# Values' projections in halves and an earlier divide at the start, half output tiles at the end, eight buffers of x

## The reference

```
Q = x @ w_q.T;  K = ctx @ w_k.T;  V = ctx @ w_v.T          (split in 16 heads of 32)
attn = softmax(Q K^T / sqrt(32))                            (64 keys for each row)
out = (attn V) @ w_o.T + b_o + x
y = (out - mean) * rsqrt(var + 1e-5) * ln_gamma + ln_beta
```

## Time and profile before

| | us |
|---|---|
| three runs: lowest, median, highest | 577.16, 578.68, 580.47 |
| the profiled execution | 577.46 |
| its span, first to last instruction | 575.7 |
| PE busy in it | 539.5 (94%) |
| DVE busy | 462.1 (80%) |
| POOL busy | 428.6 (74%) |
| ACT busy | 394.6 (69%) |

### The profile page before, as it was taken

The page is one execution under the profiler, slowest core; times in us unless marked ns, Lnnn a source line. Parts: engine busy times, 40 slices in busy tenths (PEclk is TensorE's granted clock), DMA queues, the critical chain, the costliest instruction groups (busy, mean ns, idle before and its releaser), DMA issues.

```text
span 575.7 us, 12718 instructions
## 1 busy us (share of the span) xinstructions
PE 539.5 (94%) x4522; PEld 379.5 (66%) x4522; DVE 462.1 (80%) x870; ACT 394.6 (69%) x735; POOL 428.6 (74%) x397
## 2 busy tenths in 40 slices
PE   8899879999999999999999999999999999998771
PEld 7566457676777676677677776767776776775450
DVE  7767549888889888889888889888888888888534
ACT  7537647777777777777777777777777777666522
POOL 0804466888888888888888898878888888666575
PEclk9999899999999999999999999999999999999876
DMA  9335314343344433443244433343344322222212
GB/s 323 117 89 146 99 28 135 97 130 96 117 127 121 128 97 94 127 123 119 74 124 126 117 118 117 97 130 98 123 125 126 101 72 77 82 83 64 71 64 91
DMA packets 74111, 63.23 MB, mean 110 GB/s; under 512 B 46528, under 2 KB 46528, under 8 KB 74048
## 3 DMA queue, kind: packets, MB, share of 16 engines
q1 hardware_dynamic: 74048, 62.42, 36.3%
HBM read 39.58 MB, written 16.78 MB: 98 GB/s over the span
## 4 chain that ended last, share of the span: by engine, by line
PE 81%; DVE 5%; DMA 4%; POOL 3%; issue 2%; SPq 2%; ACT 2%; POOLq 0%; ACTq 0%; DVEq 0%
PE ps_o L403 27%; PE ps_q L397 26%; PE ps_c L362 10%; PE ps_s L335 7%; DMA max_rows<-max_turned 3%; PE ps_q L275 3%; PE ps_s L345 3%; PE ps_o L275 2%; SPq L209 2%; PE ps_s L275 2%; POOL y L847 1%; POOL y L845 1%; DMA x_raw<-in_x 1%; PE ps_c L282 1%; DVE q_lo L636 1%
## 5 line engine op out<-in xcount | busy, mean ns | idle before, releaser
L397 PE MATMUL ps_q<-x_hi,wq_lo 64*128 64x512 f32 x448 | 187.0, 417 | 0.0
L403 PE MATMUL ps_o<-wo_hi,c_lo 64*128 64x512 f32 x448 | 185.9, 415 | 0.0
L397 PE MATMUL ps_q<-x_hi,wq_hi 64*128 64x512 f32 x448 | 175.9, 393 | 0.0
L397 PE MATMUL ps_q<-x_lo,wq_hi 64*128 64x512 f32 x448 | 175.4, 391 | 0.0
L403 PE MATMUL ps_o<-wo_hi,c_hi 64*128 64x512 f32 x448 | 175.0, 391 | 0.0
L403 PE MATMUL ps_o<-wo_lo,c_hi 64*128 64x512 f32 x448 | 173.2, 387 | 0.0
L397 PEld LDWEIGHTS ps_q<-x_hi,wq_lo 64*128 64x128 f32 x448 | 82.5, 184 | 66.8 <-DVE z L720 46.1
L845 POOL TENSOR_TENSOR y<-y,gamma_row 128x512 f32<-128x512 f32 x62 | 79.9, 1289 | 62.2 <-ACT y L540 62.2
L817 POOL TENSOR_TENSOR x_lo<-xT_raw,x_hi 128x512 fp32r<-128x512 f32 x60 | 77.5, 1291 | 35.3 <-ACT x_hi L475 28.4
L823 POOL TENSOR_TENSOR c_lo<-c_raw,c_hi 128x512 fp32r<-128x512 f32 x64 | 82.6, 1291 | 19.4 <-ACT c_hi L475 19.4
L397 PEld LDWEIGHTS ps_q<-x_hi,wq_hi 64*128 64x128 f32 x448 | 82.6, 184 | 9.3
(11 more groups left out here) (97 smaller groups left out, 1101.9 us busy)
## 6 DMA issues: line engine op xcount, KB each, us to landing
xT_raw<-in_xT SPq DMA_DIRECT2D x64, 256.0 KB, 3.3
x_raw<-in_x SPq DMA_DIRECT2D x64, 256.0 KB, 2.9
out<-y SPq DMA_DIRECT2D x64, 256.0 KB, 2.3
max_rows<-max_turned SPq DMA_DIRECT2D x256, 16.0 KB
ctx_raw<-in_ctxT SPq DMA_DIRECT2D x4, 256.0 KB, 4.0
wk_raw<-in_wkT SPq DMA_DIRECT2D x4, 256.0 KB, 4.2
wq_raw<-in_wqT SPq DMA_DIRECT2D x4, 256.0 KB, 5.2
wv_raw<-in_wvT SPq DMA_DIRECT2D x4, 256.0 KB, 6.6
```

The lines of the kernel that those rows point to most:

```text
L397: return nc.tensor.matmul(ps_q[:, 0, :], w[l][half, k, dims], x_[r][half, qc % 2, k, :], start=(half is lower and k == 0 and step == 0), s ...
L403: return nc.tensor.matmul(ps_o[:, 0, :], cx[l][half, k, tile], wo[r][half, k, :], start=(half is upper and k == 0 and step == 0), stop=(ha ...
```

## The change

At the start, `project_values` is called in halves of k: the first half of the first one before the first scores, and then one half in each of slots 0 to 6, ahead of `subtract_max` and not behind it. `divide` moves ahead of `queries_to_lo` on DVE. `max_rows` gets two buffers, and with them two semaphores. `x_raw` and the small tiles of the norm get eight buffers; x is loaded earlier (slots 2 to 5, and `load_x(t)` in the loop in place of `load_x(t - 4)`), and no load of x is left in the tail. In the tail the output tiles go in halves around `score`, `subtract_max` and `combine_values`; tiles 62 and 63 go to banks of ps_s; DVE finishes tiles 57, 58, 62 and 63 in place of 62 and 63.

```diff
-    BY_DVE = 2
+    BY_VECTOR = (57, 58, 62, 63)
...
-        max_rows = sb("max_rows", [P, CHUNK], fp32r)
+        max_rows = sb("max_rows", [P, 2, CHUNK], fp32r)
-        x_raw = sb("x_raw", [P, 4, DM], fp32)
+        x_raw = sb("x_raw", [P, 8, DM], fp32)
...
         def out_bank(i):
+            if i >= TILES - 2:
+                return ps_s[:, i % 2, :]
...
             def load_x(i):
-                wait(sp, z_done, i - 3)
+                wait(sp, z_done, i - 7)
             def fill_max_rows(n):
-                wait(sp, shifted_done, n)
+                wait(sp, shifted_done, n - 1)
...
-                if t in (2, 3):
+                if 2 <= t <= 5:
                     load_x(2 * t - 4)
                     load_x(2 * t - 3)
...
-            for t in range(OUT_LAG + 1, SLOTS + 1):
-                load_x(t - 4)
+            for t in range(OUT_LAG + 1, SLOTS):
+                load_x(t)
...
-            for i in range(SLOTS - OUT_LAG - 1, TILES):
-                if i + 5 < TILES:
-                    load_x(i + 5)
+            fill_max_rows(SLOTS - 1)
+            for i in (55, 57, 56, 58, 59, 60, 62, 61, 63):
                 store(i)
```

PE, the start:

```diff
             project_queries(0)
+            project_values(0, first_half)
             for t in range(OUT_LAG):
                 score(t)
                 project_queries(t + 1)
+                if t == 0:
+                    project_values(0, second_half)
+                else:
+                    project_values((t + 1) // 2, first_half if t % 2 else second_half)
                 if 1 <= t < OUT_LAG - 1:
                     subtract_max(t - 1)
-                if 1 <= t <= KT:
-                    project_values(t - 1)
                 if t >= 2:
                     combine_values(t - 2)
```

PE, the tail (the new list):

```diff
+            subtract_max(61); project_output(56, first_half); score(63)
+            project_output(56, second_half); project_output(57, range(KT)); combine_values(61)
+            project_output(58, first_half); subtract_max(62); project_output(58, second_half)
+            combine_values(62); project_output(59, first_half); subtract_max(63)
+            project_output(59, second_half); combine_values(63)
+            project_output(60, range(KT - 1)); project_output(61, range(KT - 1))
+            project_output(62, first_half); project_output(60, (KT - 1,))
+            project_output(61, (KT - 1,)); project_output(62, second_half); project_output(63, range(KT))
```

ACT, the start and the tail (the new list):

```diff
-                if 1 <= t <= KT:
-                    even_values(t - 1)
+                if t % 2 == 0:
+                    even_values(t // 2)
...
+            normalise(54); exponentiate(61); log_sums(60); invert_sums(60); negate_max(62)
+            invert_deviation(55); normalise(55); context_to_hi(60); log_sums(61); negate_max(63)
+            invert_sums(61); exponentiate(62); context_to_hi(61); log_sums(62); invert_sums(62)
+            exponentiate(63); invert_deviation(56); context_to_hi(62); normalise(56)
+            log_sums(63); invert_sums(63); invert_deviation(57); context_to_hi(63)
+            invert_deviation(58); invert_deviation(59); normalise(59); invert_deviation(60)
+            normalise(60); invert_deviation(61); normalise(61); invert_deviation(62); invert_deviation(63)
```

DVE, the start and the tail (the new list):

```diff
                 fold_halves(t)
+                if t >= 3:
+                    divide(t - 3)
                 queries_to_lo(t + 1)
                 turn_max(t)
-                if t >= 3:
-                    divide(t - 3)
-                if 1 <= t <= KT:
-                    odd_values(t - 1)
+                if t % 2 == 0:
+                    odd_values(t // 2)
...
+            statistics(55); turn_scores(62); half_maxima(62); fold_halves(62); turn_scores(63)
+            turn_max(62); divide(60); half_maxima(63); fold_halves(63); add_residual(56)
+            turn_max(63); divide(61); add_residual(57); statistics(56); add_residual(58)
+            statistics(57); divide(62); statistics(58); add_residual(59); finish(57); divide(63)
+            statistics(59); finish(58); add_residual(60); statistics(60); add_residual(61)
+            statistics(61); add_residual(62); statistics(62); finish(62)
+            add_residual(63); statistics(63); finish(63)
```

POOL, the start, the loop and the tail (the new list):

```diff
-                if t >= 5:
-                    add_bias(t - 5)
                 if t >= 3:
                     context_to_lo(t - 3)
+                if t >= 4:
+                    add_bias(2 * t - 8)
+                    add_bias(2 * t - 7)
...
-                add_bias(i + 3)
+                add_bias(t - 1)
...
+            scale(54); add_bias(62); add_bias(63); shift_mean(55); scale(55)
+            context_to_lo(60); context_to_lo(61); shift_mean(56); context_to_lo(62); scale(56)
+            context_to_lo(63)
             for i in (59, 60, 61):
                 shift_mean(i)
                 scale(i)
```

More of the change, by code:

```diff
@@ L118, in cross_attention_kernel @@
         xT_loaded = [sem(f"xT_loaded{k}") for k in range(KT)]
-        x_loaded = [sem(f"x_loaded{s}") for s in range(4)]
+        x_loaded = [sem(f"x_loaded{s}") for s in range(8)]
         x_biased = sem("x_biased")
@@ L307, in project_queries, with project_values @@
                 mm.then_inc(q_product, 1)
-            def project_values(b2):
-                wait(pe, even_values_done, 2 * b2)
-                wait(pe, odd_values_done, 2 * b2)
+            def project_values(b2, ks):
+                if ks[0] == 0:
+                    wait(pe, even_values_done, 2 * b2)
+                    wait(pe, odd_values_done, 2 * b2)
                 keys = slice(b2 * P, (b2 + 1) * P)
-                for k in range(KT):
+                for k in ks:
                     if b2 == 0:
@@ L341, in subtract_max @@
                     pe.wait_ge(select_filled, 16 * 8)
-                pe.wait_ge(max_rows_filled, 64 * (n + 1))
+                pe.wait_ge(max_rows_filled[n % 2], 64 * (n // 2 + 1))
                 for pair in range(2):
                     rows = slice(64 * pair, 64 * (pair + 1))
-                    mm = nc.tensor.matmul(ps_s[:, 2 * (n % 2) + pair, :], select[rows, :], max_rows[rows, :],
+                    mm = nc.tensor.matmul(ps_s[:, 2 * (n % 2) + pair, :], select[rows, :], max_rows[rows, n % 2, :],
                                           start=False, stop=True, skip_group_check=True)
@@ L536, in normalise @@
             def normalise(i):
[L537 to L538 removed]
+                s, c = i % 4, i % 8
+                act.wait_ge(shift_done, by_scalar(i) + 1)
                 wait(act, y_stored[s], 16 * (i // 4))
[L540 to L541 removed]
+                nc.scalar.activation(y[:, s, :], z[:, s, :], ACT.Identity, bias=shift[:, c:c + 1],
+                                     scale=rstd[:, c:c + 1]).then_inc(normed_done, 1)
             def exponentiate(n):
@@ L782, in _ @@
             statistics(57)
-            divide(SLOTS - 2)
+            divide(62)
             statistics(58)
             add_residual(59)
+            finish(57)
+            divide(63)
             statistics(59)
-            divide(SLOTS - 1)
-            for i in (60, 61):
-                add_residual(i)
-                statistics(i)
-            for i in (62, 63):
-                add_residual(i)
-                statistics(i)
-                finish(i)
+            finish(58)
+            add_residual(60)
+            statistics(60)
+            add_residual(61)
+            statistics(61)
+            add_residual(62)
+            statistics(62)
+            finish(62)
+            add_residual(63)
+            statistics(63)
+            finish(63)
         @block.gpsimd
```

214 lines of the change are left out of this document (108 added, 106 removed).

## The result

The kernel after the change takes 559.94 us (median of four runs, 559.06 to 560.87), against 577.92 for the kernel before, run beside it (median of four; the 578.68 above is that of the first three of them). The ratio is 0.9682, with a 95% interval of 0.9646 to 0.9718: about 18 us, or 3.2%, faster. The profiled execution took 559.06, its span 557.3, against 557.7 forecast for the span.

The account below looks back on a forecast made before the run. PE bounds the loop, which keeps its 440.5 us; only 33 us of idle in start and tail can be won. Start 7.1 and tail 10.9 gained: 578.68 - 18.0 = 560.7 us, range 555.5 to 566.5.

Parts of the forecast that it names:

- Rival 4: Loop: POOL's list waits for x in every slot, lengthening the period; at 0.4 us per slot 583 us; chance 0.03.
- the collision: Start: max_rows fills queue behind w_o transfers on two DMA engines, losing 3.8 of the 10.9 us gained.
- fill 3: Start: max_rows fill of slot 3 lands at about 55.3, needed at 52.8, so PE waits 2.5 us.
- fill 4: Start: max_rows fill of slot 4 lands at about 63.2, needed at 62.3, so a wait of 0.9 us.
- Rival 1: Start: no collision, fills and w_o land in time; first interleaved tile at 68.7, kernel 556.9 us; chance 0.18.
- the loop at 64.9 + 7.6: End of the start: slot 6 starts at 64.9 and the loop 7.6 later, at 72.5.
- rival 3: Start: PE at 1.2 GHz and ACT held by w_o; gains only 4, first tile at 75, 563.8 us; chance 0.13.
- the pace of 6.9: Start: from slot 2 on, a slot takes 8.28 - 1.4 = 6.9 us with values in halves.
- c_raw waits: Start: PE's waits of 2.81 and 3.25 us, from `divide` standing behind `queries_to_lo`; none over 0.3 afterwards.
- c_lo(63): Tail: done at 547.7 against 553.2 before, 5.5 us won; 27.6 after the last loop matmul.
- 12, if finish(57) does not hold divide(63) (1.5 less): Tail's upper end: gain of 12 us, if DVE's divide(63) need not wait 1.5 for finish(57) ahead of it.
- Rival 2: Tail: the new order waits for itself, two waits grow by 2.5 each; tail gains 6, 565.6 us; chance 0.20.

Follow-up runs that it names:

- the start alone: Kernel before with only the start's new order on PE, ACT and DVE, one max_rows buffer, four x buffers, old tail: 571.56 us, ratio 0.9877.
- `divide` late: Changed kernel with `divide` behind `turn_max` again in the start, values still in halves: 563.47 us, ratio 0.9744.
- values late: Changed kernel with the values' projections whole and behind `subtract_max` again, `divide` still early: 559.67 us, ratio 0.9674.
- one max_rows: Changed kernel with all fills into one max_rows buffer, the fill's wait shifted accordingly: 559.45 us, ratio 0.9688.
- the last run above: Changed kernel with w_o in transfers of 32 rows, rstd(62) ahead of normalise(61), tile 63's residual and statistics ahead of finish(62): 554.85 us, ratio 0.9606.
- the tail alone: Changed kernel with the start's order of before (values whole behind `subtract_max`, `divide` late): 567.27 us, ratio 0.9809.

## Why the prediction was right, and where its sizes were off

The total came out closer than its parts: the start gained 6.0 where 7.1 was forecast, the tail 12.1 where 10.9 was, and that the two misses nearly cancel is luck.

**The loop** kept its time: 440.23 against 440.46. Rival 4 is out.

**The start: the mechanism was right, and shown.** The slots ran at 6.98 until the fill of slot 3 was late, behind w_o. Giving w_o transfers of 32 rows removed both waits and gave 4.1 us from the first scores to the first tile, against the 3.8 that the prediction took off for the collision. The rule cited from the Trainium skill ("DMA: Bandwidth & Descriptors", the section on why a DMA increments its semaphore by 16) fits: 32 can be divided by 16, and the same bytes no longer held up what was behind them (3.1 to landing in place of 8.1 for x). Rival 1, no collision, gave 68.7 for the first tile; it became true at 69.11 only when the form of w_o was changed.

**The start's sizes.** The wait for fill 3 was 1.90 and not 2.5, for fill 4 it was 1.44 and not 0.9: their sum is 3.3 against 3.4. The rest of the 1.1 by which the start fell short (6.04 against 7.1) lies at its two ends: this execution's first queries ended 0.33 later (19.98, not 19.65), and from slot 6 to the first tile it took 8.3 where 7.6 was forecast, with 1.57 of waiting for the odd values' copy. The term that was mis-sized is "the loop at 64.9 + 7.6". Most of its 0.7 is w_o once more, by way of ACT, which waited for the last quarter of it ahead of `queries_to_hi`:

```profile
70.08 0.63 ACT L495 ACTIVATE wo_hi<-wo_raw 128x512 fp32r<-128x512 f32 x1 [1.95 <-DMA wo_raw<-in_woT]
```

DVE's low part of the queries, and all behind it in that slot, waited for that; with w_o in 32 rows the same stretch took 7.7. The forecast had put this hold of ACT at nothing and left it to rival 3.

**Rival 3** (more lost) came true in its mechanisms in some executions, and in none at its price. ACT's hold was there, as just said. Other kernels with this start's order had 2.68, 2.10 and 2.48 for the same fill. Behind the 2.68 and the 2.48 the granted clock fell (means of 0.84 and 0.72 from 55 to 60), behind the 2.10 and the 1.90 it did not. From the first scores the first tile took 52.3 and 52.0 with the fall, 51.6 and 52.1 without, so that it cost 0.7 at most, and the first tile was in none of them at the 75 of rival 3. With the fall the wait for the next fill was gone, without it it was 1.23 and 1.44: the later fill had its wait in the time that PE lost.

**Which part of the start pays** is the step that failed in its attribution. The prediction gave the pace of 6.9 to the halves and named `divide` as the cure of the c_raw waits beside them. The runs show that `divide`'s place alone gives the same first tile (73.52), and that the halves without it lose 2.7 of the gain from the first scores (3.5 by the medians). Beside the early `divide` the halves pay only once w_o is out of the way. The sum had both halves of the edit in it and needed no split between them, and so the total came out right.

**The tail** gained 12.1 where 10.9 was taken and 11.1 worked out. `finish(57)` does hold divide(63), in its place as said; its second step took 0.75, not the 1.44 taken from the earlier trace rows, since it began just ahead of POOL's step of `scale(56)`, and POOL's was the longer one for it (1.81). PE did not fall to the lower clock in this tail; in four executions of other kernels with the same PE list it did, and where nothing else differed their tails were 1.2 longer. That it stayed up here was luck. c_lo(63) was 1.3 earlier than forecast. The step "12, if finish(57) does not hold divide(63) (1.5 less)" was wrong in what it promised: with the hold taken away, in the one order that was tried, the tail was 0.8 longer. The rounds of 3.9 and 4.1 and rstd(62) behind `normalise(61)` ended last, as said; but of the 2.67 that DVE waits there only 1.1 can be had by the earlier rstd, because DVE's steps then take 1.5 longer beside POOL's. Rival 2 is out: no two waits grew.

Of the tail's 12.1, the x buffers with their earlier loads give 4.7 and the remaining 7.4 belong to the new lists with DVE's two more tiles. These were not run apart, so how the 7.4 is split between the half tiles on PE, the fill ahead of the stores and tiles 57 and 58 on DVE stays open.

## What to carry to other kernels

Look at the first dimension of every transfer: here one of 2 in place of 32 made what was issued behind it pay, and it began to cost when a faster schedule took the slack. When two edits of an order come together, price each without the other: here one moved line gave all, and the larger edit beside it paid nothing until a third thing was mended. In a tail, an earlier result on one engine is worth what the other engines' lists leave of it: look at all of them, and at which steps lengthen each other, before pricing a wait at its length. And compare stretches of single executions only where the clock and the waits ahead of them are alike.

## What the runs showed of the hardware

**DVE and POOL lengthen each other's steps.** `SCALAR_TENSOR_TENSOR` of 128x512 fp32 on DVE took 0.75 alone and up to 1.85 beside POOL's `TENSOR_TENSOR`, by how much of the two lay together; that took 1.26 to 1.30 alone and 1.58 to 1.81 beside DVE's. DVE's additions that read one operand from PSUM kept their 0.69 throughout. The Trainium skill ("SBUF — State Buffer", section "Who interferes with whom") says that a DVE instruction with two SBUF inputs contends with a GpSimd instruction that reads SBUF; it calls the ports that they share an exclusive lock. The trace agrees: in the kernel after, POOL's step runs from 549.72 to 550.98, DVE's begins at 550.09 and ends at 551.53, which is 0.55 behind POOL's end.

```profile
549.72 1.26 POOL L875 TENSOR_TENSOR y<-y,gamma_row 128x512 f32<-128x512 f32 x1 [0.93 <-ACT y L560]
551.06 1.59 POOL L877 TENSOR_TENSOR y<-y,beta_row 128x512 f32<-128x512 f32 x1
```

In the three other places of this tail where DVE's step began while one of POOL's ran (POOL's end at 534.39, 540.14 and 546.88), DVE's ended 0.54 behind it, whether it had lain beside it for long (1.70 in all) or for short (1.00). And where POOL's `TENSOR_TENSOR` began while DVE's step ran, it ended 1.12 to 1.15 behind DVE's end, as in the second line. That fits an exclusive lock: most of the later step's work comes when the other is done.

**PE's clock behind a wait.** With the new order of the start the granted clock fell behind single waits of 2.68 and 2.48 and stayed up behind 2.10 and 1.90; but it fell too behind 1.63 (the start alone: a mean of 0.66 from 65 to 70), and with `divide` late behind 1.03 and 1.22 close together (0.79 from 60 to 65). In the new tail much the same wait for the fill of slot 61, 1.65 to 1.76, was followed by the fall in four executions (values late, `divide` late, one max_rows, and the last run above) and not in six. Behind a wait of 3.25 at the end of the start it fell in the tail alone (0.75 from 80 to 85) and not in the kernel before. The length of the last wait alone does not say whether it falls.
